# Value products from three products of rounded parts in a perceiver block, with the parts made ahead by ScalarE and GpSimd

## The reference, cut to what matters

```python
# x: (32, 64, 256), ctx: (32, 1601, 256), all fp32; 16 heads of 16
kv = cond @ wkv.T + bkv                       # keys and values of 1601 context rows
k, v = jnp.split(kv, 2, axis=-1)              # v: 1601 x 256 per batch entry
attn = softmax(einsum('bnhd,bmhd->bhnm', q, k) * scale)
o = einsum('bhnm,bmhd->bnhd', attn, v)        # then a quantised projection
x = x + out                                   # then a selective scan, then a mixture of experts
```

## Time and profile before

| | |
|---|---|
| median of three runs | 2730.23 us |
| the profiled execution | 2730.2 us, span 2727.8 us (2.4 us lie around it) |
| TensorE busy | 2284.1 us, 84% |
| VectorE busy | 1787.7 us, 66% |
| ScalarE busy | 1416.3 us, 52% |
| GpSimd busy | 694.3 us, 25% |
| mean granted TensorE clock | 0.928 |
| first scores to last scores of the mixer | 53.2 to 2085.3 us |

### The profile page before, as it was taken

One profiled execution on the slowest core, in us unless ns is written; L12 is line 12 of the kernel. 1 busy time (PEld: TensorE's weight loads), 2 busy tenths in 40 slices (PEclk: granted clock), 3 DMA queues, 4 the chain that ended last, 5 costly groups with the idle time before them and its releaser, 6 DMA issues. The chain is left out here.

```text
span 2727.8 us, 56109 instructions
## 1 busy us (share of the span) xinstructions
PE 2284.1 (84%) x22152; PEld 1553.2 (57%) x22152; DVE 1787.7 (66%) x3151; ACT 1416.3 (52%) x2948; POOL 694.3 (25%) x634
## 2 busy tenths in 40 slices
PE   5998999999999989898989899999997099999200
PEld 4665666656565656565656556565664067777200
DVE  4457777767677777677777777676776545555343
ACT  1556565656566556556565656565665144444100
POOL 1113222232323132322232222323231300000576
PEclk9999999999999999999999999999998599999655
DMA  3344412020101011111111120201010167777443
GB/s 139 149 163 172 147 39 78 27 76 31 72 32 72 32 72 37 66 45 59 47 57 66 50 90 26 78 31 72 29 48 20 49 221 243 248 245 248 137 121 112
DMA packets 90193, 255.27 MB, mean 94 GB/s; under 512 B 12240, under 2 KB 46672, under 8 KB 87888
## 3 DMA queue, kind: packets, MB, share of 16 engines
q1 hardware_dynamic: 77648, 218.13, 22.7%
q0 software_dynamic: 12288, 33.57, 3.9%
HBM read 163.31 MB, written 88.34 MB: 92 GB/s over the span
## 5 line engine op out<-in xcount | busy, mean ns | idle before, releaser
L774 ACT ACTIVATE sb_probsT<-W 128x512 f32<-128x512 f32 (+1 forms) x1024 | 471.9, 511 | 413.0 <-PE W L612 410.5
L784 ACT ACTIVATE sb_probs<-S,sb_negmax 128x1604 f32<-128x1604 f32 x256 | 409.0, 1598 | 251.9 <-DVE sb_negmax L941 251.4
L612 PE MATMUL W<-sb_ident,sb_probs 128*128 128x128 f32 (+1 forms) x3328 | 483.0, 283 | 50.5 <-DVE sb_z L1015 50.2
L941 DVE TENSOR_REDUCE sb_negmax<-S 128x1 f32<-128x1604 f32 x256 | 465.9, 1820 | 11.3 <-PE S L602 11.3
L612 PEld LDWEIGHTS W<-sb_ident,sb_probs 128*128 128x128 f32 (+1 forms) x3328 | 355.7, 140 | 167.2 <-issue 104.0
L574 PE MATMUL W<-sb_ctx,sb_wkv_in 128*32 128x401 f32 x4096 | 417.3, 528 | 32.8 <-DVE sb_V L936 27.7
L584 PE MATMUL W<-sb_wkv_in,sb_ctx 128*128 128x256 f32 (+1 forms) x1664 | 417.9, 394 | 21.8 <-DVE sb_K_lo L926 18.7
L627 PE MATMUL O<-sb_probsT,sb_V 128*32 128x128 f32 (+1 forms) x6656 | 332.5, 280 | 40.9 <-ACT sb_probsT L774 39.1
L627 PEld LDWEIGHTS O<-sb_probsT,sb_V 128*32 128x32 f32 (+1 forms) x6656 | 209.6, 110 | 254.1 <-issue 176.9
L926 DVE SCALAR_TENSOR_TENSOR sb_K_lo<-W,sb_pair_cols,sb_K_hi 128x401 fp32r<-128x401 f32 x256 | 162.0, 633 | 280.6 <-ACT sb_K_hi L766 280.4
L584 PEld LDWEIGHTS W<-sb_wkv_in,sb_ctx 128*128 128x128 f32 (+1 forms) x1664 | 299.0, 190 | 81.6 <-DVE sb_K_lo L926 25.9
(11 more groups left out here) (185 smaller groups left out, 3073.5 us busy)
## 6 DMA issues: line engine op xcount, KB each, us to landing
sb_ctx<-ctxT SPq DMA_DIRECT2D x32, 1604.0 KB, 6.7
xe_scratch<-sb_none SPq DMA_DIRECT2D x32, 1024.0 KB, 14.8
sb_BC<-bc_scratch SPq DMA_DIRECT2D x16, 2048.0 KB, 7.1
sb_xg<-xe_scratch SPq DMA_DIRECT2D x64, 512.0 KB, 4.6
y_scratch<-sb_ys SPq DMA_DIRECT2D x64, 512.0 KB, 3.2
sb_wgu<-wgu SPq DMA_DIRECT2D x64, 192.0 KB, 4.5
sb_wd<-wdT SPq DMA_DIRECT2D x64, 96.0 KB, 1.9
sb_x_q<-x SPq DMA_DIRECT2D x16, 128.0 KB, 2.3
```

The lines of the kernel that those rows point to most:

```text
L612: ins = pe.transpose(W[0:keys_in(t), n * P:(n + 1) * P], probs[(slot - 1) % 2][:, t * P:t * P + keys_in(t)], ident[:])
L774: act.activation(probsT[a % 2][0:keys, 0:n], ring[bank_of(i, "T", slot, a)][0:keys, 0:n], ACT.Copy)\
L784: act.activation(probs[slot % 2][:].rearrange("p (c k) -> p c k", c=QUADS), scores_of, ACT.Exp, bias=negmax[:, slot:slot + 1], accum_out=d ...
L941: dve.tensor_reduce(negmax[:, slot:slot + 1], scores_of, AX.XY, ALU.max, negate=True).then_inc(max_done, 1)
```

## The change

The value weight and the context are each parted into a rounded fp32r part and the rest (also fp32r), and v is made of three products: high by high, high by low, low by high. ScalarE makes the high part of a unit of context (`part_high`), GpSimd the low part by a subtraction (`part_low`), two slots ahead of the unit's product, into three buffers. The GpSimd list is rewritten by slots, so that a part of each slot has its place in it; `scan_input` is cut into halves, and a part stands between the two halves of the first. At the start the weight is parted once.

```diff
+V_PARTS = 3
+        wv_hi, wv_lo = (sb(f"wv_{m}", [P, DT, D], F32R) for m in ("hi", "lo"))
+        part_hi, part_lo = ([sb(f"part_{m}{n}", [P, DT, 2 * P], F32R) for n in range(V_PARTS)] for m in ("hi", "lo"))
...
+        def parted_in(i, slot, cur, nxt):
+            slot += 2
+            if slot >= SLOTS:
+                i, slot, cur, nxt = i + 1, slot - SLOTS, nxt, i < PAIRS - 2
+            v = values_in(slot)
+            if v and cur and (v[0] or nxt):
+                yield part_of(i, *v), v[0], v[1], 16 * (i + 2 - v[0])
...
@@ def _(pool) @@
+            def part_low(part, b, unit, loaded):
+                keys = keys_of_unit(unit)
+                n = keys.stop - keys.start
+                pool.wait_ge(part_hi_up, part + 1)
+                pool.tensor_tensor(part_lo[part % V_PARTS][:, :, 0:n], ctx_t[b][:, :, keys], part_hi[part % V_PARTS][:, :, 0:n].bitcast(F32),
+                                   ALU.subtract).then_inc(part_lo_up, 1)
...
             def body(i, cur, prev, nxt):
+                for slot in range(SLOTS):
+                    if slot == 0 and cur:
+                        spread_q(i, 1)
+                    if slot == 1 and not early(i):
+                        scatter(i - 2)
+                    if slot == 2 and prev:
...
+                    if slot == 3 and cur and nxt:
+                        rstd_q(i + 1)
+                    if slot == 4 and cur:
+                        spread_q(i, 2)
+                    if slot == 5 and prev:
+                        scan_input(i - 1, 0, 0)
+                    if slot == 8 and cur:
+                        spread_q(i, 3)
+                    if slot == 8 and prev:
+                        scan_input(i - 1, 1, 0)
+                    if slot == 9 and prev:
+                        scan_input(i - 1, 1, 1)
+                    if slot == 11 and cur and nxt:
+                        spread_q(i + 1, 0)
+                    if slot == 13 and prev:
...
+                    for part in parted_in(i, slot, cur, nxt):
+                        part_low(*part)
+                    if slot == 5 and prev:
+                        scan_input(i - 1, 0, 1)
...
@@ def _(pe) @@
             def v_mm(i, b, unit):
                 W = take(i, "V", b, unit)
-                pe.wait_ge(ctx_in[b], 16 * (1 if round_of(i) == "start" else i + 2 - b))
+                part = part_of(i, b, unit)
+                pe.wait_ge(part_lo_up, part + 1)
+                hi, lo = part_hi[part % V_PARTS], part_lo[part % V_PARTS]
+                products = [(x, w, k) for x, w in ((hi, wv_hi), (hi, wv_lo), (lo, wv_hi)) for k in range(DT)]
                 for n, t in enumerate(V_UNITS[unit]):
-                    for k in range(DT):
-                        ins = pe.matmul(W[0:keys_in(t), n * D:(n + 1) * D], ctx_t[b][:, k, t * P:t * P + keys_in(t)],
-                                        wkv_in[:, k, D:2 * D], start=(k == 0), stop=(k == DT - 1))
+                    for m, (x, w, k) in enumerate(products):
+                        ins = pe.matmul(W[0:keys_in(t), n * D:(n + 1) * D], x[:, k, n * P:n * P + keys_in(t)],
+                                        w[:, k, :], start=(m == 0), stop=(m == len(products) - 1))
...
@@ def _(act) @@
+            def part_high(part, b, unit, loaded):
+                keys = keys_of_unit(unit)
+                act.wait_ge(ctx_in[b], loaded)
+                if part >= V_PARTS:
+                    i, *job = user_of(part - V_PARTS)
+                    act.wait_ge(ring_full, full_at(i, "V", *job))
+                act.activation(part_hi[part % V_PARTS][:, :, 0:keys.stop - keys.start], ctx_t[b][:, :, keys], ACT.Copy).then_inc(part_hi_up, 1)
...
                     if cur and (slot < 12 or nxt):
                         k_up(i, slot)
+                    for part in parted_in(i, slot, cur, nxt):
+                        part_high(*part)
```

More of the change, by code:

```diff
@@ L288, in mixer_phase @@
         ctx_in = [sem(f"ctx_in{n}") for n in range(2)]
+        part_hi_up = sem("part_hi_up")
+        part_lo_up = sem("part_lo_up")
+        wv_up = sem("wv_up")
         x_in = sem("x_in")
@@ L354, in next_step, with part_of, user_of, keys_of_unit @@
             return divmod((slot // STRIPS + 1) % STEPS, 2)
+        def part_of(i, b, unit):
+            n = len(V_UNITS)
+            return unit if round_of(i) == "start" else n + i * 2 * n + (0 if b else n) + unit
+        def user_of(part):
+            n = len(V_UNITS)
+            if part < n:
+                return -1, 0, part
+            i, rest = divmod(part - n, 2 * n)
+            return (i, 1, rest) if rest < n else (i, 0, rest - n)
+        def keys_of_unit(unit):
+            return slice(V_UNITS[unit][0] * P, V_UNITS[unit][-1] * P + keys_in(V_UNITS[unit][-1]))
+        def parted_in(i, slot, cur, nxt):
[5 more added lines that the diff above has]
+                yield part_of(i, *v), v[0], v[1], 16 * (i + 2 - v[0])
         def keys_of(i, slot):
@@ L467, in spread_q, with scan_input @@
                 pool.tensor_tensor(Q_lo[j % 2][:], Q_own[:], Q_hi[j % 2][:].bitcast(F32), ALU.subtract).then_inc(q_up, 1)
-            def scan_input(p, h):
-                for half in range(2):
+            def part_low(part, b, unit, loaded):
[4 more added lines that the diff above has]
+                                   ALU.subtract).then_inc(part_lo_up, 1)
+            def scan_input(p, h, half):
+                if True:
                     if h == 0:
@@ L493, in scatter @@
                         ln3[:], None, bounds_check=E * CAP - 1, oob_is_err=False).then_inc(scattered, 16)
+            pool.wait_ge(wv_up, 1)
+            pool.tensor_tensor(wv_lo[:], wkv_in[:, :, D:2 * D], wv_hi[:].bitcast(F32), ALU.subtract).then_inc(wv_up, 1)
             rstd_q(0)
+            for unit in range(3):
+                part_low(unit, 0, unit, 16)
             spread_q(0, 0)
+            for unit in range(3, len(V_UNITS)):
+                part_low(unit, 0, unit, 16)
+            part_low(len(V_UNITS), 1, 0, 16)
@@ L498, in body @@
             def body(i, cur, prev, nxt):
[L499 to L520, removed]
+                for slot in range(SLOTS):
[4 more added lines that the diff above has]
+                    if slot == 2 and prev:
+                        pool.wait_ge(dve_up, dve_at(i - 1, "V2"))
+                        pool.tensor_tensor(st[:, 9:10], st[:, 8:9], neg_half[:], ALU.pow).then_inc(pool_up, 1)
+                    if slot == 3 and cur and nxt:
[13 more added lines that the diff above has]
+                    if slot == 13 and prev:
+                        pool.wait_ge(dve_up, dve_at(i - 1, "V3"))
+                        pool.tensor_tensor(st[:, 17:18], st[:, 16:17], neg_half[:], ALU.pow).then_inc(pool_up, 1)
+                    for part in parted_in(i, slot, cur, nxt):
+                        part_low(*part)
+                    if slot == 5 and prev:
+                        scan_input(i - 1, 0, 1)
@@ L544, in _ @@
             pe.wait_ge(wq_set, 4)
+            pe.wait_ge(wv_up, 2)
             pe.wait_ge(w_in, 16 * len(loads))
@@ L805, in decay @@
                     ins.then_inc(act_up, 1)
+            def part_high(part, b, unit, loaded):
[5 more added lines that the diff above has]
+                act.activation(part_hi[part % V_PARTS][:, :, 0:keys.stop - keys.start], ctx_t[b][:, :, keys], ACT.Copy).then_inc(part_hi_up, 1)
+            act.activation(wv_hi[:], wkv_in[:, :, D:2 * D], ACT.Copy).then_inc(wv_up, 1)
+            for unit in range(V_PARTS):
+                part_high(unit, 0, unit, 16)
             for slot in range(-STRIPS, 0):
                 k_up(-1, slot)
+            for unit in range(V_PARTS, len(V_UNITS)):
+                part_high(unit, 0, unit, 16)
+            part_high(len(V_UNITS), 1, 0, 16)
             def body(i, cur, prev, nxt):
```

## The result

The changed kernel takes 2779.1 us (median of four runs) beside 2730.6 for the kernel before on the same chip: ratio 1.0178, 95% interval 1.016 to 1.0195. That is 1.8% slower, and outside the predicted range. The profiled execution has a span of 2777.5 us at a mean granted clock of 0.917 (0.928 before).

A forecast was written before the change was run, and what follows sets the result against it. TensorE was taken as the bound (84% of the span), with other masters in some slots. Gains of 2.9 + 0.3 less 0.8 and 2.2 a full pair, with the other pairs, came to 9 to 10 us: 2720 us, range 2660 to 2758.

The forecast's parts named there:

- The products: Value units in slots 1 to 3 and 11 to 14: 0.42 us gained a full unit, 2.9 a pair.
- ScalarE's parts: High-part copies on ScalarE: 0.62 us each, covered by its idle time, so they cost nothing.
- GpSimd's part: Low parts on GpSimd: 1.28 us each, 14 a pair; TensorE should not wait for them.
- Slot 4: VectorE's norm_q waits for GpSimd's part_low and spread_q: 0.8 us a pair lost (0 to 1.3).
- Slot 0: VectorE's route waits for GpSimd's spread_q, delaying k_low: 2.2 us a pair lost (0 to 2.6).
- The clock: Slower rival: the pause behind slot 1's turns halves TensorE's clock, 2.6 us a pair more, 2756 us; chance 0.15.
- Slots 8 and 9: Part of slots 5 to 10, booked together at 0, from +0.9 to -0.5 us a pair, GpSimd collisions included.
- The sum: A pair with everything (2 to 14): 2.9 + 0.3 - 0.8 - 2.2 = 0.2 us gained.
- slot 15: spread_q leaves this slot, so one GpSimd collision of today goes: 0.3 us a pair gained.
- The signs: Wrong if slot 0 keeps its length, V groups take over 1.9 us, or the mixer's mean clock falls.
- Scatter: GpSimd's scatter comes about 3.5 us later but ends before the slot-2 power is due: free.
- The first rival: No GpSimd collision with route in slot 0: 31 us more gained, 2689 us; chance 0.25.

The follow-up runs named there:

- e11: The kernel of e8 run again on a chip where the kernel before took 2734.1 us: 0.965 of the kernel before, 2638.0 us.
- e10: The kernel before, without the change, with the added wait of e5 and the added matmuls of e8: 0.9797 of the kernel before.
- e3: The changed kernel with the old plain fp32 products; parts still made and waited for: 1.0361 of the kernel before.
- e5: As e1, and GpSimd also waits, behind the power of slot 3, until norm_q has ended: 0.9909 of the kernel before.
- e4: The changed kernel with 10 useless matmuls in slot 1 and 16 with zero weights in slot 4: 1.0058 of the kernel before.
- e9: The changed kernel with one wait added: GpSimd holds slot 0's spread_q until route has ended: 1.0173 of the kernel before.
- e1: The changed kernel with spread_q(i + 1, 1) moved from slot 0 to slot 14 of the pair before: 1.0004 of the kernel before.
- e7: As e5, with the third spread_q and first half of the second scan_input moved from slot 8 to slot 7: 0.9808 of the kernel before.
- e12: The kernel of e7 run again on a chip where the kernel before took 2734.1 us: 0.9746 of the kernel before.
- e6: The kernel before with only the products changed, 12 fp32r records a unit from parts made once at the start: 0.9809 of the kernel before.
- e8: As e7, with zero-weight matmuls added, 16 in slot 4 and 5 in slot 8: 0.9728 of the kernel before.

## Why the prediction was wrong

**The products (2.9 a pair).** Right in price a record (0.118, measured 0.12), too good in the step to the next group: 0.06 put in, 0.19 measured, so 0.30 a full unit and not 0.42. Of the seven slots counted six gave it; slot 13 gave nothing, as its keys now wait 0.23 us for VectorE's copy of V (L1009). Slots 5, 6 and 10, booked at 0, gave 0.26 to 0.30, and slot 7 took 0.31 back through ScalarE's list. Together 2.3 to 2.4 a pair, and e11 against e10 says the same.

**ScalarE's parts.** Right: 0.62 us each, and free (e3).

**GpSimd's part (1.28 us, TensorE doesn't wait for it).** Right: the full units take 1.30 in the mean, and no wait of TensorE is put down to them.

**Slot 4 (-0.8, bound 1.3).** The mechanism was right, the place and the size were not: 1.37 by the table, just above the bound. The low part blocks L976 for 1.38 (1.12 before), as foreseen; but Q_lo meets L933, which was blocked before too, and the new victim is L932, behind Q_hi. L934, the one foreseen for Q_lo, keeps its 0.35. e5 shows that all of slot 4's loss and 1 us of the old length are this.

**Slot 0 (-2.2, bound 2.6): the step that failed.** The term priced the collision as a wait alone and put the clock behind it at nothing. Measured, it is 4.7 us a pair (slot 1, 11.95 against 7.27): 2.7 of wait and 2.0 of clock, by e4. The wait was nearly right in size, with two errors against each other. The forecast took Q_hi and Q_lo at their whole lengths, 2.4; L1190 lasts 1.02 and 1.29 beside them, which is 0.7 and 1.0 more than its own 0.28, so `route` is pushed back by 1.7 and not 2.4. And the chain wasn't followed on: it runs into the next low part, at 1368.28, which I had put beside the maximum. That is the third block, 1.1 us more than L1193's own 0.17. The three come to 2.9; less the slack of 0.28 that is 2.6, and the wait is 2.5 in the row. By my estimate, 2779 - 14 x 2.0, that wait without the clock would have left the program at 2751, inside the range.

**The clock.** It stood among the rivals at 0.15, priced at 2.6 a pair on top of the forecast. It came true in seven of eleven pairs at 3.0 each, 2.0 in the mean. I weighed it down by slot 8, where 5.45 busy of 7.30 leave the clock at 1.00; no pause of TensorE there is longer than 1.5. The nearer row was the earlier trace rows: a pause of 3.5 in one piece and 0.50 behind it. But the length of the pause doesn't settle it either: 2.50 (once 2.74) is followed by 1.00 in four pairs, and the 1.44 of slot 9 by a fall in none of eleven pairs (e9), four (the changed kernel) or all (e1). What else decides stays open. The rival's own time, 2756, was still short of the result, since it stood on the forecast's small slot terms.

**Slots 8 and 9 (booked 0, +0.9 to -0.5).** +0.52, and with e1's times +1.5. The list puts Q_own to Q_lo a low part later, and `scan_input` behind them, so that times_c and the last sum of slot 9 are blocked, K_lo comes 2.6 us after the scores and not 1.2, and in some pairs the clock falls. e7 and e12 bring slot 9 to 8.02 by two lines moved from slot 8 to slot 7; 7.61 (e6) is what it takes without parts.

**The sum.** Foreseen 0.2 us gained a pair; by the table 3.9 lost, 4.1 to be explained. The products and slot 15 gave 2.7 and not 3.2 (0.5); the wait of slot 1 took 2.7 and not 2.2 (0.5); its clock took 2.0 and not 0; slot 4 took 0.6 more; slot 9 0.5. That is 4.1, and the clock of slot 1 is half of it.

**The signs.** Two of the three named for a wrong forecast came. Slot 0 kept its 5.62 us: the late K_lo frees the bank for work of slot 1, so the loss stands there, 4.4 for the two slots and not 1.8. And the clock's mean fell, in the whole span from 0.928 to 0.917.

**Scatter.** Free, as written, in the changed kernel; e9 shows what it costs when its cover is gone: slot 3 grows by 4.9 us a pair, the blocked L1134 and the clock included.

The Trainium skill ("SBUF — State Buffer", two separate sides) says that GpSimd and a VectorE instruction with two SBUF inputs shut each other out. By that rule L1190 and L1193 had to wait, and the trace agrees (1.29 for 0.28, 1.28 for 0.17). The first rival, no collision in slot 0, is refuted by these rows.

## What to carry to other kernels

Before work is put on GpSimd, follow VectorE's list on past the first collision: a delayed chain runs into the next GpSimd instruction, and the pause it leaves on TensorE can be paid a second time by the clock (2.7 us and 2.0 here). The low parts themselves did little harm once the list around them was put right: in e11 the change gives 2.4 us a pair, all that the products were worth. The same change went from 1.018 to 0.965 of the kernel before by three places in a list, one wait and 21 useless matmuls a pair. And try such cures on the kernel before as well (0.980), or the change gets the credit for them.

## What the runs showed of the hardware

- A matmul of zero weights into a bank in use is a working way to keep TensorE's clock: in slot 4, 16 of them (0.23 us each) keep it at 1.00 through the pause; the slot went from 12.49 to 10.94 us with no other change in it, and slot 5 from 7.79 to 7.27 (e12, e11).
- The length of a pause doesn't tell whether the clock falls behind it. In the changed kernel 2.50 us are followed by 0.50 in seven pairs, and 2.50 us (once 2.74) by 1.00 in the other four. Slot 9 has a pause of 1.44 us in every pair of e9, of the changed kernel, of e4, e3 and e1; the clock falls in 0, 4, 8, 10 and 11 of eleven. e1, e4 and e9 change nothing in the slots 8 and 9 themselves, so part of what an edit wins in one slot can be lost to the clock in another.
- The kernel before already lost by the clock: in 5 of its pairs slot 9 takes 10.9 us in place of 7.91, from a granted clock of 0.61 in its first 4 us, with no pause longer than 1.5 us in the slot ahead. e10 removes all of them.
```profile
891.56:895.60 4.04, 4.04 (x29) 3.77 (x29) 3.01 (x5) 2.95 (x8) 2.36 (x1) 0.61 0.00 0
```

- On one chip the kernel before took some 100 us longer. In the four traces from it (e5 to e8) TensorE waits in slots 1 and 2, many times with "issue" as the only reason, and slot 2 of e7 takes 15.46 us at a granted clock of about 0.7, where the same kernel has 7.92 on another chip (e12). From e7's trace there:

```profile
972.39 1.03 PE L672 MATMUL W<-sb_ident,sb_probs 128*128 128x128 f32 x4 [0.69 <-issue]
973.83 0.89 PE L672 MATMUL W<-sb_ident,sb_probs 128*128 128x128 f32 x3 [0.41 <-issue]
975.20 0.69 PE L706 MATMUL W<-sb_ident,sb_o_tok 128*128 128x128 f32 x2 [0.48 <-issue]
```

  What holds the instructions back there stays open; no run took it apart.
